# A fused transformer block on one core: the third normalisation moved out of the tokens and into the softmax

## The chip, the cores and the metric

The kernel runs on one core of one Trainium2 chip. Its time is the device time of one execution in microseconds (us). TensorE (PE in the profile, with PEld for its weight loads), VectorE (DVE), ScalarE (ACT), GpSimd (POOL) and SyncE (SP) run their own instruction streams and wait for each other by semaphores; only the DMA queues move data to and from memory.

## The reference, cut to what matters

Four residual steps on `x` of 4 x 2048 tokens x 512, all in fp32. The change concerns the third: attention of the normalised tokens to 77 context rows each sequence, with a ReLU projection on both sides.

```python
x = x + tanh(g_xattn[0]) * L0_xattn(ctx, layernorm(x), conv_w, conv_b, 1024, 1024, 4)
x = x + tanh(g_ffn[0]) * L0_ffn(layernorm(x), weight, bias)          # quantised linear layer
x = x + tanh(g_xattn[1]) * L1_xattn(layernorm(x), p_mask, ctx, q_mask, ctx, U_w, D_param)
x = x + tanh(g_ffn[1]) * L1_ffn(layernorm(x), Wr, W1, W2)            # 8 experts with a capacity

def layernorm(x, eps=1e-5):
    return (x - mean(x)) / sqrt(var(x) + eps)

def L1_xattn(passage, p_mask, question, q_mask, rep, U_w, D_param):
    Up = relu(einsum('bpi,hi->bph', passage, U_w))
    Uq = D_param[0] * relu(einsum('bqi,hi->bqh', question, U_w))
    scores = where(q_mask[:, None, :], -inf, einsum('bph,bqh->bpq', Up, Uq))
    return einsum('bpq,bqh->bph', softmax(scores, axis=2), rep)
```

## The kernel before

After a setup the kernel has two stages. The token stage (about 0 to 872 us) takes the tokens in 16 groups of 512 (four tiles of 128 tokens) through a pipeline of six stages, called z, a, b, c, d and e in the code. In one step the group of stage z is loaded, that of a is normalised and quantised (norms "a" and "b"), that of b goes through the quantised linear layer and gets the third norm (kind "c"), c is the attention projection with the scores, d the softmax and the attention's result, e the fourth norm (kind "d"), the router and the payload for the experts. The expert stage (872 us to the end) follows.

There are 21 steps. Steps 0 to 5 and 16 to 20 are written out, and steps 6 to 15 are a loop at run time (`Fori`, L210) on every engine. In the loop an address that turns with the group, such as a tile of `X`, comes from a register. Nothing schedules the kernel: each engine has a function `body(z, a, b, c, d, e)` in which the order of its work is written by hand, and every instruction waits for counters of others. A wait is a queue's head: what stands behind it on its engine waits too.

The places that the change touches, with their lines in this kernel:

- Third norm. VectorE takes `bn_stats` of each tile of `X` (`st_c`, L924), aggregates (`mv_c`, L928) and later makes the shift `nb_c` (L934). ScalarE makes `rs_c` by a logarithm `lv_c` (L555) and an exponential (L557), then writes four normalised tiles `n2` (L562; the profile calls this output `n`). TensorE turns `n2` by transposes against an identity (L718) in two pairs, and ScalarE and VectorE split the turned tiles into a high part `n2T_hi` (L574) and a low part `n2T_lo` (L1006).
- Linear layer. Four products of `wd` with the turned input `xdT` (TensorE, L710); VectorE adds each to `X` (`add_linear`, L974).
- Projection. Four products of `uw` with `n2T` (TensorE, L780), each relu'd by ScalarE into `up_hi` (`up(0)` to `up(3)`, L583), the low part `up_lo` by VectorE (L997).
- Softmax. VectorE takes the maximum `smx` over each row of scores (L1011) and subtracts it into `sc` (L1013), ScalarE takes one exponential over all four tiles, `al` (L601), TensorE turns it (L816), ScalarE and VectorE split it into `alT_hi` (L605) and `alT_lo`, and VectorE sums it into `ssm` (L1024) for the factor `scf`.
- GpSimd adds a bias to the whole group of `X` (L488), and SyncE loads the groups of `xs` and `X`.

`xs` is the shifted input of norm "a"; ScalarE writes its four normalised tiles (L638), which need `nb_a` (L1062) and the mask product `a_m` (L1059) of VectorE.

## Time and profile before

| | |
|---|---|
| Median of 3 runs | 2196.72 us (2196.54 to 2197.13) |
| The profiled execution, its own time | 2196.92 us |
| Its span (first to last instruction) | 2194.6 us |
| Mean granted TensorE clock | 0.961 |
| Busy: PE, PEld | 1982.1 us (90%), 1692.3 us (77%) |
| Busy: DVE, ACT, POOL | 1043.4 us (48%), 794.8 us (36%), 670.9 us (31%) |
| Token stage, then experts | 0 to 872 us, 872 to 2194.6 us |

The busy times are those of the whole span. The two stages have different limits, so they say little of one step of the token stage: for that the timeline of one step is read, engine by engine. All rows are of one execution.

### The profile page before, as it was taken

Reading aid. Unit: us, or ns where it says so; the run is one execution under the profiler, and the core shown is the slowest. Engines: PE = TensorE matmul, PEld = TensorE weight load, DVE = VectorE, ACT = ScalarE, POOL = GpSimd, SP = SyncE. Lnnn points to the kernel's source line nnn. Section 1 sums busy time; section 2 is a strip of 40 time slices with the busy share of each in tenths; the row PEclk is TensorE's granted clock in tenths of the full one; section 3 lists DMA queues with packets and bytes.
Section 4 is the critical chain, followed back from the end, with each engine's and each line's share of the span. In section 5 each row is a group of like instructions: output and inputs, shape, how many; then the busy total and the mean of one; then the engine's idle time right before and its main releaser. Section 6 shows DMA issues by size and latency. Waiting matters only on the chain.

```text
span 2194.6 us, 35464 instructions
## 1 busy us (share of the span) xinstructions
PE 1982.1 (90%) x11356; PEld 1692.3 (77%) x11357; DVE 1043.4 (48%) x2321; ACT 794.8 (36%) x1548; POOL 670.9 (31%) x579
## 2 busy tenths in 40 slices
PE   4468998899889975799999999999999999999997
PEld 2456776677667754698988998899889899899986
DVE  3478888998899744424241115122413313322241
ACT  1254656555665443324141114111413313311241
POOL 0534243434353302415051115111513313301250
PEclk9689999999999985899999999999999999999999
DMA  6311333333333423615051004201512403301130
GB/s 190 112 61 43 122 130 121 116 120 140 115 120 121 146 85 117 197 32 185 20 183 43 29 29 156 69 29 38 183 43 91 129 29 96 120 19 38 54 112 16
DMA packets 152243, 208.41 MB, mean 95 GB/s; under 512 B 12831, under 2 KB 78623, under 8 KB 152198
## 3 DMA queue, kind: packets, MB, share of 16 engines
q1 hardware_dynamic: 111125, 114.14, 16.3%
q0 software_dynamic: 15728, 43.38, 6.5%
q10 hardware_dynamic: 25344, 50.33, 6.3%
q8 instruction: 22, 0.36, 0.1%
q14 instruction: 24, 0.19, 0.0%
HBM read 140.98 MB, written 68.37 MB: 95 GB/s over the span
## 4 chain that ended last, share of the span: by engine, by line
PE 58%; ACT 0%; issue 0%; DMA 0%; POOL 0%; POOLq 0%; DVEq 0%; ACTq 0%; DVE 0%
PE bank L1646 23%; PE bank L1654 22%; PE bank L1619 5%; PE bank L1599 5%; PE bank L1577 1%; PE bank L1608 1%; DMA tg<-t_d,idx_t 0%; ACT w_hi L1510 0%; PE bank L1583 0%; ACT w_hi L1511 0%; POOLq L1351 0%; DMA slots<-slot_d 0%; POOL out_dram L1389 0%; DVEq L1292 0%; ACT inT_hi L1496 0%
## 5 line engine op out<-in xcount | busy, mean ns | idle before, releaser
L1737 DVE SCALAR_TENSOR_TENSOR hT_lo<-bank,hT_hi 128x256 fp32r<-128x256 f32 x352 | 149.0, 423 | 657.0 <-ACT hT_hi L1541 657.0
L1541 ACT ACTIVATE hT_hi<-bank 128x256 fp32r<-128x256 f32 x352 | 135.1, 384 | 747.8 <-PE bank L1646 747.8
L1646 PE MATMUL bank<-inT_hi,w_lo 128*128 128x256 f32 x1408 | 398.5, 283 | 0.0
L1646 PE MATMUL bank<-inT_lo,w_hi 128*128 128x256 f32 x1408 | 398.3, 283 | 0.0
L1646 PE MATMUL bank<-inT_hi,w_hi 128*128 128x256 f32 x1408 | 396.8, 282 | 0.0
L1654 PE MATMUL bank<-w_hi,hT_hi 128*128 128x512 f32 x704 | 279.9, 398 | 0.0
L1646 PEld LDWEIGHTS bank<-inT_hi,w_hi 128*128 128x128 f32 x1408 | 269.0, 191 | 13.3
L1646 PEld LDWEIGHTS bank<-inT_lo,w_hi 128*128 128x128 f32 x1408 | 269.0, 191 | 12.0
L1654 PE MATMUL bank<-w_lo,hT_hi 128*128 128x512 f32 x704 | 277.7, 394 | 0.0
L1654 PE MATMUL bank<-w_hi,hT_lo 128*128 128x512 f32 x704 | 274.1, 389 | 0.0
L1646 PEld LDWEIGHTS bank<-inT_hi,w_lo 128*128 128x128 f32 x1408 | 269.0, 191 | 0.0
L1389 POOL DMA_INDIRECT out_dram<-ob,idx_x x46 | 46.5, 1010 | 633.9 <-DVE ob L1747 617.5
L1399 POOL TENSOR_TENSOR w_lo<-stage,w_hi 128x512 fp32r<-128x512 f32 x112 | 159.9, 1444 | 79.8 <-ACT w_hi L1510 79.7
L1654 PEld LDWEIGHTS bank<-w_hi,hT_lo 128*128 128x128 f32 x704 | 132.3, 188 | 30.1
L1654 PEld LDWEIGHTS bank<-w_hi,hT_hi 128*128 128x128 f32 x704 | 133.5, 190 | 17.4
L1654 PEld LDWEIGHTS bank<-w_lo,hT_hi 128*128 128x128 f32 x704 | 133.6, 190 | 15.2
L718 PE MATMUL bank<-ident,n 128*128 128x128 f32 x512 | 79.8, 290 | 72.0 <-POOL n L494 40.3
L469 POOL DMA_INDIRECT slot_d<-pay,flat x64 | 62.6, 979 | 266.2 <-DVE flat L959 251.6
L494 POOL TENSOR_TENSOR n<-q,s 128x512 f32<-128x512 fp8e4 x64 | 83.5, 1332 | 188.0 <-DVE q L1108 188.0
L1711 DVE TENSOR_TENSOR w_lo<-stage,w_hi 128x512 fp32r<-128x512 f32 x128 | 133.3, 1054 | 0.0
L718 PEld LDWEIGHTS bank<-ident,n 128*128 128x128 f32 x512 | 59.9, 148 | 93.8 <-issue 66.1
L780 PE MATMUL bank<-n2T_hi,uw_hi 128*128 128x512 f32 x256 | 110.2, 430 | 13.3 <-DVE up_lo L997 13.3
(266 smaller groups left out, 3931.5 us busy)
## 6 DMA issues: line engine op xcount, KB each, us to landing
stage<-in_L_ffn_W_dram SPq DMA_DIRECT2D x256, 256.0 KB, 3.6
X<-in_x_dram SPq DMA_DIRECT2D x16, 1024.0 KB, 5.3
t_d<-tt ACTq DMA_DIRECT2D x16, 1024.0 KB, 4.4
x_d<-x ACTq DMA_DIRECT2D x16, 1024.0 KB, 6.7
out_dram<-y ACTq DMA_DIRECT2D x16, 1024.0 KB, 4.3
xs<-in_x_dram SPq DMA_DIRECT2D x16, 768.0 KB
cw_a<-in_L_xattn_conv_w_dram SPq DMA_DIRECT2D x2, 1024.0 KB, 17.1
cw_b<-in_L_xattn_conv_w_dram SPq DMA_DIRECT2D x2, 1024.0 KB, 18.8
```

Source lines behind the costliest of these rows:

```text
L469: pool.indirect_dma_start(out=slot_d, out_offset=bass.IndirectOffsetOnAxis(ap=flat[:, j:j + 1], axis=0), in_=pay[:, j, :], in_offset=None, ...
L494: pool.tensor_tensor(n1[:, j, :].rearrange("p (n c) -> p n c", c=BLK), q8[:, j, :].rearrange("p (n c) -> p n c", c=BLK), s64[:, j, :].unsq ...
L718: last = pe.transpose(dst_bank[:, k * P:k * P + P], src[:, j, k * P:k * P + P], ident[:, :])
L780: last = pe.matmul(u_banks[h % 2][:, :], l, rows_t, start=(k == 0 and n == 0), stop=(k == KB - 1 and n == 2))
L1399: pool.tensor_tensor(w1_lo[:, :, fs], w1_block(f), w1_hi[:, :, fs].bitcast(F32), ALU.subtract).then_inc(e_split[f % RING], 1)
L1541: act.activation(hT_hi[:, f % 4, :], hb[f % 4][:, 0:CN], ACT.Relu).then_inc(e_hh, 1)
L1599: last = pe.matmul(first_bank[q % 2][:, :], l[:, k, :], r[:, k, qs], start=(n == 0), stop=(n == 3 * KB - 1))
L1619: last = pe.matmul(unit_acc[:, :], l[:, q % 2, f, :], r[:, q * FQ + f, :], start=(q == 0 and n == 0), stop=(q == NF - 1 and n == 3 * FQ - 1))
L1646: last = pe.matmul(hb[f % 4][:, 0:CN], l[:, k, fs], r[:, k, :], start=(n == 0), stop=(n == 3 * KB - 1))
L1654: last = pe.matmul(acc[i][:, :], l[:, f % 4, js], r[:, f, :], start=(f == 0 and n == 0), stop=(f == FB - 1 and n == 2))
L1711: dve.tensor_tensor(w2_lo[:, f, :], w2_block(f), w2_hi[:, f, :].bitcast(F32), ALU.subtract).then_inc(e_split[f % RING], 1)
L1737: dve.scalar_tensor_tensor(out=hT_lo[:, f % 4, :], in0=hb[f % 4][:, 0:CN], scalar=0.0, in1=hT_hi[:, f % 4, :].bitcast(F32), op0=ALU.max, o ...
```

## The change

The kernel computes the same function by another route. A token's normalised row is (X - mean) * rs. The mean goes out of the tokens if every row of the projection weight is centred once: then `X` itself can be projected. The scale `rs` is positive, so it passes the ReLU and can be applied to the scores, in the exponential.

- Setup: ScalarE sums and centres the projection weight `uf`. The keys' side needs the uncentred weight, so TensorE sums the keys over the features (`keysum`) and VectorE adds the mean times that sum back, three instructions for each part instead of one. The mask's bias gets a factor that is zero where every key is masked.
- The third norm's `st_c`, `mv_c` and `nb_c` go. VectorE's `add_linear` also writes the sum of each row (`sum_c`), and one small instruction makes `nm_c`, the negative mean. ScalarE writes no `n2`: four squares of `X` with bias `nm_c` write their row sums `sq_c` (their full output goes to `junk`), and `lv_c` and `rs_c` follow these instead of standing ahead of `up(1)`.
- TensorE turns `X`, once all four `add_linear` are done; `x2T_hi` and `x2T_lo` take the place of `n2T`. Its loop over the steps is written out, that of the other engines isn't.
- Softmax: VectorE multiplies `smx` by -`rs_c` (`nbx`, 128x4) instead of subtracting; ScalarE's exponential reads the scores in four instructions of 128x77 with bias `nbx`, scale `rs_c` and the row sum `ssm` written by the way. TensorE waits for each tile. The router's product waits for the exponentials, not for VectorE.
- Scratch of the expert planner that lay in `n2` lies in `X`.

The diff, cut to its core:

```diff
@@ -144,12 +144,13 @@
-        for kind in "abcd":
+        for kind in "abd":
...
+        sum_c, nm_c, sq_c, rs_c = small("sum_c", T), small("nm_c", T), small("sq_c", T), small("rs_c", T * T)
...
-        smx, ssm, srd, scf = small("smx", T), small("ssm", T), small("srd", T), small("scf", T)
+        smx, nbx, ssm, srd, scf = (small(n, T) for n in ("smx", "nbx", "ssm", "srd", "scf"))
...
@@ -325,8 +328,8 @@
-        plan = n2[0:1, :, :].rearrange("o i d -> o (i d)")
-        onesc = n2[:, T - 1, 0:P]
+        plan = X[0:1, 0:T, :].rearrange("o i d -> o (i d)")
+        onesc = X[:, T - 1, 0:P]
...
@@ -537,7 +540,7 @@
-            pool.wait_ge(p_ct, T * NG)
+            pool.wait_ge(v_x3, T * (NG - T + 1))
             pool.iota(cidx, [[1, CI]], base=0, channel_multiplier=0,
...
@@ -597,8 +600,11 @@
-                    wait(act, v_sm, 4 * d + 2)
-                    act.activation(al[:, :, :], sc[:, :, :], ACT.Exp).then_inc(a_al, 1)
+                    wait(act, v_sm, 3 * d + 2)
+                    settled(act)
+                    for j in range(T):
+                        act.activation(al[:, j, :], p_sc[:, j, :], ACT.Exp, bias=nbx[:, j:j + 1],
+                                       scale=rs_c[:, ds((d % T) * T + j, 1)], accum_out=ssm[:, j:j + 1]).then_inc(a_al, 1)
                 if d is not None:
...
@@ -637,19 +643,26 @@
                                        scale=a_sc[:, j:j + 1]).then_inc(a_u, 1)
-                if b is not None:
-                    rstd("c", b)
                 up(1)
...
                 if b is not None:
-                    wait(act, v_ln["c"], LN * (b + 1))
-                    wait(act, p_ct, T * b)
-                    normed("c", n2, lambda j: X[:, ds((b % T) * T + j, 1), :], a_n2)
+
+                    wait(act, v_nm, b + 1)
+                    wait(act, a_sq, T * b)
+                    settled(act)
+                    for j in range(T):
+                        act.activation(junk[:, j, :], X[:, ds((b % T) * T + j, 1), :].rearrange("p o d -> p (o d)"),
+                                       ACT.Square, bias=nm_c[:, j:j + 1], accum_out=sq_c[:, j:j + 1]).then_inc(a_sq, 1)
+                    wait(act, a_sq, T * (b + 1))
+                    act.activation(lv["c"][:, :], sq_c[:, :], ACT.Ln, bias=eps[:, :], scale=1.0 / D).then_inc(a_rs["c"], 1)
+                    wait(act, a_rs["c"], 2 * b + 1)
+                    settled(act)
+                    act.activation(rs_c[:, ds((b % T) * T, T)], lv["c"][:, :], ACT.Exp, scale=-0.5).then_inc(a_rs["c"], 1)
                 up(3)
...
                     act.activation(re_[:, :, :], rd[:, :, :], ACT.Exp).then_inc(a_re, 1)
-                turned_hi(n2T_hi, n_banks, p_ct, b, a_ch, p_cu, 0, 2)
+                turned_hi(x2T_hi, n_banks, p_ct, b, a_ch, p_cu, 0, 2)
                 if e is not None:
...
@@ -679,6 +692,17 @@
             body(*groups(0))
+            act.wait_ge(ready, 1)
+            act.activation(onesr[:, :], onesf[:, :], ACT.Copy).then_inc(k_act, 1)
+            act.wait_ge(l_uf, 16)
+            for k in range(KB):
+                act.activation(uf[:, k, :], uf[:, k, :], ACT.Copy, accum_out=us[:, k:k + 1]).then_inc(k_act, 1)
+            act.wait_ge(k_act, act_at[f"us{KB - 1}"])
+            act.activation(unm[:, :], us[:, :], ACT.Copy, scale=-1.0 / D).then_inc(k_act, 1)
+            act.activation(umean[:, :], us[:, :], ACT.Copy, scale=1.0 / D).then_inc(k_act, 1)
+            act.wait_ge(k_act, act_at["unm"])
+            for k in range(KB):
+                act.activation(uf[:, k, :], uf[:, k, :], ACT.Identity, bias=unm[:, k:k + 1]).then_inc(k_act, 1)
             for k in range(KB):
...
@@ -758,7 +782,7 @@
-                        wait(pe, v_sm, 4 * d + 2)
+                        wait(pe, a_al, T * (d + 1))
...
@@ -776,7 +800,7 @@
-                                                                        n2T_hi[:, k, :], n2T_lo[:, k, :])):
+                                                                        x2T_hi[:, k, :], x2T_lo[:, k, :])):
...
@@ -786,12 +810,15 @@
                     if b is not None:
-                        wait(pe, a_n2, T * b + j + 1)
                         if j < 2:
-                            wait(pe, v_x2, T * b + 3 + j)
+                            wait(pe, v_x2, T * (b + 1))
                         else:
                             wait(pe, v_cl, T * b + j - 1)
-                        turn(n_banks[j % 2], n2, j).then_inc(p_ct, 1)
+                        for k in range(KB):
+                            last = pe.transpose(n_banks[j % 2][:, k * P:k * P + P],
+                                                X[:, (b % T) * T + j, k * P:k * P + P],
+                                                ident[:, :])
+                        last.then_inc(p_ct, 1)
...
@@ -811,8 +838,8 @@
                 if d is not None:
-                    wait(pe, a_al, d + 1)
                     for j in range(T):
+                        wait(pe, a_al, T * d + j + 1)
                         last = pe.transpose(b_s[0:L, j * P:j * P + P], al[:, j, :], ident[:, :])
...
@@ -888,6 +915,12 @@
+            pe.wait_ge(k_dve, dve_at["cxT3"])
+            for k in range(KB):
+                for c in (cxT_hi, cxT_lo):
+                    last = pe.matmul(bank[bank_of["keysum"]][:, 0:B * L], onesr[:, :], c[:, k, :],
+                                     start=(k == 0 and c is cxT_hi), stop=(k == KB - 1 and c is cxT_lo))
+            last.then_inc(k_pe, 1)
             for h in range(KB):
...
@@ -905,7 +938,8 @@
             prepared(pe)
-            pipeline(pe, body, 2)
+            for t in range(2, STEPS):
+                body(*groups(t))
...
@@ -971,8 +1005,10 @@
                     xb = tile_of(b, j).rearrange("p o d -> p (o d)")
+                    if j == 0:
+                        wait(dve, v_nm, b)
                     dve.scalar_tensor_tensor(out=xb, in0=l_banks[j % 2][:, :], scalar=gates[:, 2:3], in1=xb,
-                                             op0=ALU.mult, op1=ALU.add).then_inc(v_x2, 1)
+                                             op0=ALU.mult, op1=ALU.add, accum_out=sum_c[:, j:j + 1]).then_inc(v_x2, 1)
...
@@ -1009,9 +1045,11 @@
                     dve.tensor_reduce(smx[:, :], p_sc[:, :, :], AX.X, ALU.max).then_inc(v_sm, 1)
-                    wait(dve, v_sm, 4 * d + 1)
-                    dve.tensor_tensor(sc[:, :, :], p_sc[:, :, :], smx[:, :].unsqueeze(2).to_broadcast([P, T, L]),
-                                      ALU.subtract).then_inc(v_sm, 1)
+                    wait(dve, v_sm, 3 * d + 1)
+                    wait(dve, a_rs["c"], 2 * (d + 1))
+                    settled(dve)
+                    dve.scalar_tensor_tensor(out=nbx[:, :], in0=smx[:, :], scalar=-1.0, in1=rs_c[:, ds((d % T) * T, T)],
+                                             op0=ALU.mult, op1=ALU.mult).then_inc(v_sm, 1)
                 if e is not None:
...
@@ -1020,11 +1058,9 @@
                 if d is not None:
-                    wait(dve, a_al, d + 1)
-                    dve.tensor_reduce(ssm[:, :], al[:, :, :], AX.X, ALU.add).then_inc(v_sm, 1)
-                    wait(dve, v_sm, 4 * d + 3)
+                    wait(dve, a_al, T * (d + 1))
                     dve.reciprocal(srd[:, :], ssm[:, :]).then_inc(v_sm, 1)
-                    wait(dve, v_sm, 4 * d + 4)
+                    wait(dve, v_sm, 3 * d + 3)
                     dve.tensor_scalar(scf[:, :], srd[:, :], gx[:, ds(d, 1)], None, ALU.mult).then_inc(v_scf, 1)
...
@@ -1063,11 +1099,10 @@
                     wait(dve, v_x2, T * (b + 1))
-                    moments("c", b, lambda j: tile_of(b, j))
+                    wait(dve, a_sq, T * b)
+                    dve.tensor_scalar(nm_c[:, :], sum_c[:, :], -1.0 / D, None, ALU.mult).then_inc(v_nm, 1)
                 add_attention(3)
                 up_rest(1)
-                if b is not None:
-                    shift("c", b)
                 if e is not None:
...
@@ -1194,8 +1226,12 @@
                 dve.wait_ge(k_pe, pe_at[f"uq{h}"])
-                step(f"uqf{h}", dve.tensor_scalar(uqf[:, h, :], bank[bank_of[f"uq{h}"]][:, 0:B * L], 0.0,
-                                                  dp[:, h:h + 1], ALU.max, ALU.mult))
+                step(f"uqm{h}", dve.tensor_scalar(uqf[:, h, :], bank[bank_of["keysum"]][:, 0:B * L], umean[:, h:h + 1],
+                                                  None, ALU.mult))
+                after(f"uqm{h}")
+                step(f"uqa{h}", dve.tensor_tensor(uqf[:, h, :], bank[bank_of[f"uq{h}"]][:, 0:B * L], uqf[:, h, :], ALU.add))
+                after(f"uqa{h}")
+                step(f"uqf{h}", dve.tensor_scalar(uqf[:, h, :], uqf[:, h, :], 0.0, dp[:, h:h + 1], ALU.max, ALU.mult))
             low_parts("wd", wd_hi, wd_lo, D)
```

In the order of each engine's instructions this moves rows at three places. The first is ScalarE in a written-out step ahead of the loop, from norm "a" to the turned tiles (`X`, `xs` are the group's tiles, `bank` a PSUM bank). Before:

```order
L557 ACTIVATE rs_a<-lv_a 128x4
L638 ACTIVATE xs<-xs,nb_a,a_sc 128x512 x4
L555 ACTIVATE lv_c<-mv_c,eps 128x4
L557 ACTIVATE rs_c<-lv_c 128x4
L583 ACTIVATE up_hi<-bank 128x512 x2
L562 ACTIVATE n<-X,nb_c,rs_c 128x512 x4
L583 ACTIVATE up_hi<-bank 128x512
```

The same place of ScalarE after the change:

```order
L560 ACTIVATE rs_a<-lv_a 128x4
L644 ACTIVATE xs<-xs,nb_a,a_sc 128x512 x4
L586 ACTIVATE up_hi<-bank 128x512 x2
L654 ACTIVATE junk,sq_c<-X,nm_c 128x512 x4
L657 ACTIVATE lv_c<-sq_c,eps 128x4
L660 ACTIVATE rs_c<-lv_c 128x4
L586 ACTIVATE up_hi<-bank 128x512
```

The logarithm and the exponential moved from ahead of the second and third `up_hi` to ahead of the fourth, and the squares stand where the normalisations stood.

The second is VectorE in the same step, from norm "a" to the quantisation. Before:

```order
L1062 SCALAR_TENSOR_TENSOR nb_a<-mv_a,a_m 128x4
L924 BN_STATS st_c<-X 128x6 x4
L928 BN_AGGR mv_c<-st_c 128x2 x4
L987 SCALAR_TENSOR_TENSOR x<-bank,scf,X 128x512
L997 SCALAR_TENSOR_TENSOR up_lo<-bank,up_hi 128x512
L934 SCALAR_TENSOR_TENSOR nb_c<-mv_c,rs_c 128x4
L997 SCALAR_TENSOR_TENSOR up_lo<-bank,up_hi 128x512
L1095 TENSOR_REDUCE ab<-n 128x16 x4
```

The same place of VectorE after:

```order
L1098 SCALAR_TENSOR_TENSOR nb_a<-mv_a,a_m 128x4
L1103 TENSOR_SCALAR nm_c<-sum_c 128x4
L1023 SCALAR_TENSOR_TENSOR x<-bank,scf,X 128x512
L1033 SCALAR_TENSOR_TENSOR up_lo<-bank,up_hi 128x512 x2
L1130 TENSOR_REDUCE ab<-n 128x16 x4
```

Eight instructions on `X` became one of 128x4, and the shift is gone: nothing is left between the second and the third `up_lo`.

The third is VectorE at the softmax, at the start of a step. Before:

```order
L1011 TENSOR_REDUCE smx<-bank 128x4
L1013 TENSOR_TENSOR sc<-bank,smx 128x308
L924 BN_STATS st_d<-x 128x6 x4
L928 BN_AGGR mv_d<-st_d 128x2 x4
L1020 TENSOR_TENSOR alT_lo<-bank,alT_hi 77x512
L974 SCALAR_TENSOR_TENSOR X<-bank,gates,X 128x512
L1024 TENSOR_REDUCE ssm<-al 128x4
L1026 RECIPROCAL srd<-ssm 128x4
```

The same place of VectorE after:

```order
L1047 TENSOR_REDUCE smx<-bank 128x4
L1051 SCALAR_TENSOR_TENSOR nbx<-smx,rs_c 128x4
L958 BN_STATS st_d<-x 128x6 x4
L962 BN_AGGR mv_d<-st_d 128x2 x4
L1058 TENSOR_TENSOR alT_lo<-bank,alT_hi 77x512
L1010 SCALAR_TENSOR_TENSOR X,sum_c<-bank,gates,X 128x512
L1062 RECIPROCAL srd<-ssm 128x4
```

A 128x4 product took the place of the subtraction, the row sum went to ScalarE, and `add_linear` got its second output.

## Rows read from the trace of the kernel before

**Rows 1.** Busy time by stretch: start:end, length, busy (xinstructions), clock, DMA share, GB/s.

```profile
300.00:698.00 398.00, 356.59 (x1917) 281.88 (x1917) 354.20 (x889) 242.37 (x432) 163.92 (x90) 1.00 0.35 123
872.00:2194.60 1322.60, 1284.56 (x7800) 1144.07 (x7800) 388.84 (x657) 349.68 (x754) 367.18 (x388) 0.99 0.26 81
```

**Rows 2.** Timeline of VectorE, one step: start, length, instruction [idle before <-releaser].

```profile
425.20 0.69 DVE L997 SCALAR_TENSOR_TENSOR up_lo<-bank,up_hi 128x512 fp32r<-128x512 f32 x1
...
436.53 0.47 DVE L1011 TENSOR_REDUCE smx<-bank 128x4 f32<-128x308 f32 x1
437.03 0.48 DVE L1013 TENSOR_TENSOR sc<-bank,smx 128x308 f32<-128x308 f32 x1
...
458.17 1.82 DVE L1059 TENSOR_TENSOR a_m<-rs_a,mg 128x4 f32<-128x4 f32 x1 [0.77 <-ACT rs_a L557]
...
460.38 2.47 DVE L924 BATCH_NORM_STATS2 st_c<-X 128x6 f32 x4
462.77 0.41 DVE L928 BATCH_NORM_AGGREGATE mv_c<-st_c 128x2 f32<-128x6 f32 x4
...
464.87 0.15 DVE L934 SCALAR_TENSOR_TENSOR nb_c<-mv_c,rs_c 128x4 f32<-128x4 f32 x1
...
469.46 0.69 DVE L997 SCALAR_TENSOR_TENSOR up_lo<-bank,up_hi 128x512 fp32r<-128x512 f32 x1
```

**Rows 3.** Timeline of TensorE in the same step.

```profile
435.55 0.49 PE L710 MATMUL bank<-wd_hi,xdT_hi 128*128 128x512 f32 x1
...
438.40 0.60 PE L816 MATMUL bank<-ident,al 128*77 128x128 f32 x4
438.75 0.48 PE L710 MATMUL bank<-wd_hi,xdT_hi 128*128 128x512 f32 x1
...
464.05 0.40 PE L780 MATMUL bank<-n2T_hi,uw_lo 128*128 128x512 f32 x1
```

**Rows 4.** Timeline of ScalarE in the same step.

```profile
437.54 0.46 ACT L601 ACTIVATE al<-sc 128x308 f32<-128x308 f32 x1 [1.91 <-DVE sc L1013]
...
448.65 0.81 ACT L562 ACTIVATE n<-X,nb_b,rs_b 128x512 f32 x1 [1.20 <-DVE nb_b L934]
...
460.38 2.94 ACT L638 ACTIVATE xs<-xs,nb_a,a_sc 128x512 f32<-128x512 f32 x4 [2.41 <-DVE nb_a L1062]
463.22 0.29 ACT L555 ACTIVATE lv_c<-mv_c,eps 128x4 f32<-128x4 f32 x1
463.54 0.20 ACT L557 ACTIVATE rs_c<-lv_c 128x4 f32<-128x4 f32 x1
463.65 0.58 ACT L583 ACTIVATE up_hi<-bank 128x512 fp32r<-128x512 f32 x1
464.48 0.60 ACT L583 ACTIVATE up_hi<-bank 128x512 fp32r<-128x512 f32 x1 [0.25 <-PE bank L780]
465.29 2.94 ACT L562 ACTIVATE n<-X,nb_c,rs_c 128x512 f32 x4 [0.21 <-DVE nb_c L934]
468.13 0.57 ACT L583 ACTIVATE up_hi<-bank 128x512 fp32r<-128x512 f32 x1
```

**Rows 5.** Waits from 345 to 698 us: who for whom, us in total, times, longest.

```profile
DVE up_lo L997 <- ACT up_hi L583: 21.4, 16, 2.4
```

**Rows 6.** Timeline of GpSimd in the same step.

```profile
455.39 4.56 POOL L488 TENSOR_TENSOR X<-X,gbias 128x2048 f32 x1
```

**Rows 7.** ScalarE and VectorE in the first of the two last steps with a projection.

```profile
730.46 2.92 ACT L562 ACTIVATE n<-X,nb_c,rs_c 128x512 f32<-128x512 f32 x4
...
733.89 0.69 DVE L997 SCALAR_TENSOR_TENSOR up_lo<-bank,up_hi 128x512 fp32r<-128x512 f32 x1
```

**Rows 8.** VectorE in the third step of the pipeline.

```profile
119.77 2.46 DVE L924 BATCH_NORM_STATS2 st_c<-X 128x6 f32<-128x512 f32 x4
...
123.35 1.86 DVE L1095 TENSOR_REDUCE ab<-n 128x16 f32<-128x512 f32 x3
```

**Rows 9.** VectorE at the end of the setup.

```profile
86.06 2.47 DVE L924 BATCH_NORM_STATS2 st_a<-xs 128x6 f32<-128x512 f32 x4 [9.43 <-DMA xs<-comp_d]
```

49 lines of the change are left out of this document (27 added, 22 removed).

## The prediction

> **What bounds the kernel now.** I read three views: busy time by stretch, the chain of waits in the steady stretch, and the timeline of one step, engine by engine. By stretch [rows 1] the change can only act ahead of 872 us: the experts behind it take 1322.6 us at a clock of 0.99, and none of their instructions is touched. In the stretch 300 to 698 TensorE is busy 356.6 and VectorE 354.2 of 398 us, so neither is alone the bound; a step has to be followed round.
>
> A step takes 44.26 us: the fourth `up_lo` of a step starts at 425.20 and again at 469.46 [rows 2]. The same work can be followed as a ring. TensorE starts the first linear product at 435.55 and goes on without a wait of note through the four linear products, the attention and projections 0 to 2; the last matmul of projection 2 starts at 464.05 and its bank is full at 464.45 [rows 3]. ScalarE then writes `up_hi` at 464.48, the four normalised tiles at 465.29 (2.94 us) and the last `up_hi` at 468.13, done at 468.70 [rows 4]. VectorE writes the last `up_lo` at 469.46 [rows 2], 0.76 us after that was ready, since VectorE itself came late. Behind it stand the quantisation and the low parts, 10.3 us until TensorE starts the next step. So the ring is TensorE, then VectorE, with ScalarE 0.76 us behind being the bound. VectorE has slack elsewhere: for earlier `up_hi` it waits on ScalarE 16 times in 8 steps, 21.4 us, at the longest 2.4 [rows 5].
>
> **The change, part by part.** Each sum is for one step.
>
> *Moments of the third norm (VectorE).* Removed: four statistics (2.47 us), four aggregates (0.41 us) and the shift (0.15 us); added is one 128x4 instruction of about 0.15. That is 2.8 us less on VectorE between 460.38 and 464.87 [rows 2]. It is nearly all hidden: what VectorE does next needs the second `up_hi`, and ScalarE reaches that only after its four `xs` instructions (460.38 to 463.32 [rows 4]), which themselves wait for `a_m`. `a_m` cannot come earlier either: it is a 128x4 instruction of 1.82 us that ends at 459.99, when GpSimd's 4.56 us addition ends at 459.95 [rows 2, 6]. VectorE gains the 0.45 us of `lv_c` and `rs_c`, which move behind the third `up_hi`, and the shift. So VectorE could start the last `up_lo` about 0.5 us earlier, and the question is whether ScalarE lets it.
>
> *Squares, logarithm and exponential (ScalarE).* The four normalisations become four squares with a bias pointer, a number as scale, and an accumulated sum. Start to start a normalisation takes 0.71 ((2.94 - 0.81)/3, 0.81 being one's length [rows 4]). A pointer operand costs 0.09: `lv_c` with a bias takes 0.29, `rs_c` without takes 0.20 [rows 4]. So a square is 0.62, plus the accumulated sum, call it r. No row shows r. From below it is 0; from above 0.32, the distance from `lv_c` to the `rs_c` that depends on it [rows 4]. The nearest row is a small instruction behind another: `rs_c` starts 0.11 before the `up_hi` that follows it. I take r = 0.13, because reading a sum must wait for the last column. From the third `up_hi` to the last there now lie 0.49 + 3 x 0.75 + (0.71 + 0.13) for the squares, 0.34 for the logarithm, 0.35 for the exponential with its wait, less 0.10 of overlap: 4.17 us, where it was 3.65. That is +0.52.
>
> In the Trainium skill, "ScalarE: Activation LUTs", section What ACT_TABLE_LOAD costs, a pointer operand adds about 93 ns and back-to-back instructions overlap by about 93 ns; this trace agrees, with 0.09 and 0.10. "VectorE: DVE Perf Modes", section Two Vector instructions with no wait between them, says of the other engine that an instruction which also writes its accumulator is two instructions; no run here shows it yet, and it speaks for an r above nothing.
>
> *Exponential of the scores.* Before, `smx` ends at 437.00, `sc` at 437.51, ScalarE's one 128x308 `al` runs from 437.54 to 438.00, and TensorE takes it at 438.40, 0.4 us later [rows 2 to 4]. The subtraction goes (0.48 us), a 128x4 product comes (0.15 us, behind two waits, until about 437.3), and `al` becomes four 128x77 instructions with two pointers and a sum. The first starts about 0.27 after its release, as the normalisation at 465.29 does after the `nb_c` that ends at 465.02 [rows 2, 4], because its operand is addressed by a register: 437.56. One takes 0.20 + 77 x (0.46 - 0.20)/304 + 2 x 0.09 = 0.45, start to start 0.35 + r = 0.48. The fourth ends at 437.56 + 1.44 + 0.58 = 439.58. TensorE's last transpose of the four then starts near 439.7 and the second linear product near 439.8, where it was 438.75 [rows 3]: +1.07 us on TensorE, on the ring. The sum over the rows that VectorE saves lies in its slack, and is worth nothing.
>
> *TensorE turns X itself.* The first two turnings no longer wait for ScalarE's normalised tiles; in a steady step they stand behind projection 3 in TensorE's order and TensorE has no wait there, so nothing is gained. Projection 3 still waits for the second `up_lo`, now earlier than TensorE arrives. TensorE's loop is written out. The trace of before shows no such thing in the loop, but a wait that needs a register took 0.27 (above) where `al` followed `sc` in 0.03 [rows 2, 4]; TensorE may win between 0 and 0.24 for each wait that is late. I take 0.1 on the ring.
>
> *The sum of a steady step.* The last `up_hi` starts at 464.48 + 1.07 + 4.17 = 469.72, `up_lo` at 469.72 + 0.58 + 0.03 = 470.33 instead of 469.46: +0.87, less 0.1 for the written-out waits and less 0.07 for what VectorE need not catch up, +0.7. There are eleven such steps (ten of the loop and about one of the written-out ones ahead of it): +7.7.
>
> *The last two steps with a projection.* Without a first stage, VectorE waits for nobody else: the normalised tiles start at 730.46 and the last `up_lo` at 733.89, right behind its `up_hi` [rows 7]. Here all of 1.07 + 0.52 counts: 2 x 1.6 = +3.2.
>
> *The first steps.* In the third step of the pipeline there is no projection, so the moments stand on the path: `st_c` at 119.77, `ab` at 123.35 [rows 8]. That goes but for one small instruction: -3.4. The next gives -0.4.
>
> *The setup.* ScalarE sums and centres the projection weight (eight 128x512 and three small instructions: 8 x 0.6 + 3 x 0.2 = 5.4 us by the lengths in [rows 4]), TensorE adds 8 matmuls, VectorE 8 instructions of 128x308 and two small ones, 3.8 us on VectorE for the eight at the 0.48 of `sc` [rows 2]. VectorE idles 9.43 us ahead of 86.06 for a transfer that none of it feeds [rows 9]. I put it at nothing; with that cover gone it would be +4.
>
> Together 7.7 + 3.2 - 3.4 - 0.4 = +7.1 us on the profiled execution, which took 2196.9 (its span is 2194.6); the median of the runs is 2196.7, so I forecast 2203.8.
>
> **Rivals.** *The sum is nearly free.* If r is 0.02, the exponentials end 0.55 us earlier and the squares take 0.55 less: 1.1 us a step, and the steady step is shorter by 0.4 us. Eleven steps give -4.4, the last two +1.0, the first two -3.8: 2189.7, faster. For it: nothing but that a sum rides along with the data; against it, every instruction in the rows costs at least 0.1. It decides below r = 0.05.
>
> *Even.* With r near 0.08 the steady step gains or loses 0.3 at most and the last steps pay back what the first ones won: some 2199 us, within the 0.2% (4.4 us) that a measurement of this kernel can tell. For it: the nearest row, 0.11, is close.
>
> *The read drains the engine.* If the sum waits for its instruction to end and is then an instruction of 0.2 itself, with the overlap lost, r is 0.2 to 0.3. Each 0.1 more costs 0.4 in the exponentials and 0.4 in the squares: thirteen steps x 0.8 = +10 us per 0.1. At r = 0.2 the kernel takes 2211, at 0.3 2221. The row for it is the 0.32 from `lv_c` to `rs_c`.
>
> *The moments matter after all.* If ScalarE could run ahead, VectorE's 2.8 us a step would be worth up to 13 x 2.5 = 32 us. The rows of ScalarE and GpSimd [rows 4, 6] speak against it: the four `xs` wait for GpSimd.
>
> **How the numbers follow.** The forecast (r from 0.09 to 0.16, 2200 to 2208) 0.36, a dearer read 0.21, even 0.22, nearly free 0.17, the last 0.04. Slower by over 0.2% is the forecast's and the dearer read's, 0.55; within it 0.25, with a part of the forecast's low end; faster 0.20. The range 2189 to 2214 leaves out the ends of the dearest and of the last rival.
>
> **What would show it.** In the steady step: ScalarE's four `al` ending near 439.6 in the old step's count, TensorE waiting 1 us ahead of them; the squares 0.75 apart; VectorE waiting for the last `up_hi` instead of being late; a step of about 45.0 us. A gap of under 0.65 between squares would make the forecast wrong, as would a step under 44.3. The step from 93 to 127 us should shrink by 3.4, and 86.06 should stand. If the two last steps don't grow, the logarithm and exponential are not where I put them.

## The result and the profile after

| | before | after |
|---|---|---|
| Median of the runs | 2196.63 us (2196.30 to 2197.13, 4 runs) | 2211.78 us (2208.61 to 2213.12, 4 runs) |
| Span of the profiled execution | 2194.6 us | 2211.4 us |
| Mean granted clock | 0.961 | 0.959 |

The ratio is 1.0067, with a 95% interval of 1.0049 to 1.0084: slower by 15 us, clear of noise. 2203.8 was forecast, with a range of 2189 to 2214.

The step's marks tell where the time went. VectorE computes the reciprocal `i` once in each step, right behind the last `up_lo`; the table gives its start, and for the last three steps that of ScalarE's `sT`.

| stretch | before, us | after, us | difference | forecast |
|---|---|---|---|---|
| start to the first `i` | 92.53 | 99.47 | +6.94 | 0 |
| the next two steps, which had the statistics on the path | 71.88 | 68.57 | -3.31 | -3.8 |
| the last two written-out steps and the first of the loop | 128.59 | 132.51 | +3.92 | +1.4 (two of the eleven steady ones) |
| nine steps of the loop | 398.36 | 404.70 | +6.34 | +6.3 |
| the last three with a projection | 125.47 | 128.75 | +3.28 | +3.2 |
| the rest, experts included | 1377.77 | 1377.40 | -0.4 | 0 |

The steady step, the first two steps and the end came out nearly as forecast. The miss is in the setup and in two written-out steps.

One thing has to be taken out of single steps first, TensorE's granted clock. Three stretches from one `i` to the next, first one of the kernel before, then two of the changed kernel (start:end, length, busy time of PE, PEld, DVE, ACT and POOL, clock, DMA share, GB/s):

```profile
246.91:293.00 46.09, 41.31 (x213) 32.39 (x213) 39.43 (x101) 27.70 (x50) 18.42 (x10) 0.96 0.34 115
```

```profile
345.47:390.62 45.15, 40.78 (x213) 32.54 (x213) 35.70 (x96) 28.28 (x60) 18.22 (x10) 0.96 0.34 117
390.62:435.53 44.91, 40.17 (x213) 31.35 (x213) 35.60 (x95) 28.28 (x60) 18.24 (x10) 1.00 0.34 118
```

A step whose clock is 0.96 has some 4 us at about the lower of TensorE's two levels (1.2 GHz; 353.5 to 357.5 in the second fence) and is longer for it. TensorE's waits ahead of that are the same as in the next step, which kept the full clock (1.67, 0.80, 0.49 and 1.15 us in both), so no wait ahead of it explains the drop. The nine steady steps have none of these before the change and two after it. At the full clock a step takes 44.26 before and 44.91 after: +0.65; the mean of all nine is 0.70 longer.

**The steady step.** VectorE's timeline (start, length, instruction), one step of the changed kernel, against [rows 2]:

```profile
479.83 0.69 DVE L1033 SCALAR_TENSOR_TENSOR up_lo<-bank,up_hi 128x512 fp32r<-128x512 f32 x1 [0.66 <-ACT up_hi L586]
...
491.15 0.47 DVE L1047 TENSOR_REDUCE smx<-bank 128x4 f32<-128x308 f32 x1
492.12 0.16 DVE L1051 SCALAR_TENSOR_TENSOR nbx<-smx,rs_c 128x4 f32<-128x4 f32 x1 [0.51 <-DVE smx L1047]
...
515.39 0.17 DVE L1103 TENSOR_SCALAR nm_c<-sum_c 128x4 f32<-128x4 f32 x1
...
518.87 0.69 DVE L1033 SCALAR_TENSOR_TENSOR up_lo<-bank,up_hi 128x512 fp32r<-128x512 f32 x1 [2.36 <-ACT up_hi L586]
...
524.74 0.69 DVE L1033 SCALAR_TENSOR_TENSOR up_lo<-bank,up_hi 128x512 fp32r<-128x512 f32 x1 [0.66 <-ACT up_hi L586]
```

The step takes 44.91 us, where it was 44.26. VectorE now waits for the last `up_hi` (0.66 us), where it came late before. The statistics are gone, and in their place VectorE waits 2.36 us ahead of the second `up_lo`. The waits in the same stretch say it in one line (total, times, longest), against 21.4 us in 16 waits [rows 5]:

```profile
DVE up_lo L1033 <- ACT up_hi L586: 41.3, 23, 2.4
```

TensorE and ScalarE in this step, against [rows 3, 4]:

```profile
490.09 0.50 PE L734 MATMUL bank<-wd_hi,xdT_hi 128*128 128x512 f32 x1 [0.20 <-DVE x2T_lo L1042]
...
493.10 1.53 PE L843 MATMUL bank<-ident,al 128*77 128x128 f32 x4
494.38 0.48 PE L734 MATMUL bank<-wd_hi,xdT_hi 128*128 128x512 f32 x1
...
519.64 0.39 PE L804 MATMUL bank<-x2T_hi,uw_lo 128*128 128x512 f32 x1
```

```profile
475.15 0.60 ACT L586 ACTIVATE up_hi<-bank 128x512 fp32r<-128x512 f32 x1 [1.24 <-PE bank L804]
475.65 0.71 ACT L654 ACTIVATE junk<-X,nm_c 128x512 f32 x1
476.26 0.19 ACT L654 ACTIVATION_READ_ACCUMULATOR junk<-X,nm_c 128x1 f32 x1
...
478.60 0.30 ACT L657 ACTIVATE lv_c<-sq_c,eps 128x4 f32<-128x4 f32 x1
479.10 0.20 ACT L660 ACTIVATE rs_c<-lv_c 128x4 f32 x1 [0.20 <-ACT lv_c L657]
479.21 0.59 ACT L586 ACTIVATE up_hi<-bank 128x512 fp32r<-128x512 f32 x1
...
492.54 0.42 ACT L606 ACTIVATE al<-bank,nbx,rs_c 128x77 f32<-128x77 f32 x1 [2.29 <-DVE nbx L1051]
...
492.95 0.41 ACT L606 ACTIVATE al<-bank,nbx,rs_c 128x77 f32<-128x77 f32 x1
...
493.73 0.41 ACT L606 ACTIVATE al<-bank,nbx,rs_c 128x77 f32<-128x77 f32 x1
494.03 0.21 ACT L606 ACTIVATION_READ_ACCUMULATOR al<-bank,nbx,rs_c 128x1 f32 x1
```

From the first to the second linear product TensorE takes 4.29 us instead of 3.20: +1.09. From the third `up_hi` to the fourth ScalarE takes 4.06 instead of 3.65: +0.41. The last `up_lo` starts 0.62 behind the start of its `up_hi` instead of 1.33: -0.71. TensorE starts 10.26 us behind the last `up_lo` instead of 10.35 (-0.09), and needs 25.65 from the second linear product to the end of projection 2 instead of 25.70 (-0.05). Together +0.65. The row sum is an instruction of its own, 0.19 us long, and adds some 0.09 to the distance of two squares (0.71 for one pointer and a sum, where 0.62 was worked out for one pointer alone).

**The setup.** VectorE and GpSimd:

```profile
64.18 0.48 DVE L1232 TENSOR_TENSOR uqf<-bank,uqf 128x308 f32<-128x308 f32 x1
64.69 7.17 DVE L1234 TENSOR_SCALAR uqf<-uqf,dp 128x308 f32<-128x308 f32 x1
...
72.86 0.38 DVE L1234 TENSOR_SCALAR uqf<-uqf,dp 128x308 f32<-128x308 f32 x1
...
85.25 2.46 DVE L958 BATCH_NORM_STATS2 st_b<-X 128x6 f32<-128x512 f32 x4
...
88.84 2.47 DVE L958 BATCH_NORM_STATS2 st_a<-xs 128x6 f32<-128x512 f32 x4
...
92.30 4.26 DVE L1095 TENSOR_TENSOR a_m<-rs_a,mg 128x4 f32<-128x4 f32 x1 [0.66 <-ACT rs_a L560]
```

```profile
58.17 5.05 POOL L532 TENSOR_TENSOR cx_hl<-cx,cx_hl 77x512 fp32r<-77x512 f32 x4 [54.92 <-ACT cx_hl L714]
63.18 4.05 POOL L536 TENSOR_TENSOR wf<-wq,wsc 128x512 f32<-128x512 fp8e4 x4
67.20 4.49 POOL L483 TENSOR_TENSOR X<-X,xs 128x2048 f32<-128x2048 f32 x1
...
92.05 4.49 POOL L491 TENSOR_TENSOR X<-X,gbias 128x2048 f32<-128x2048 f32 x1 [20.36 <-ACT n L565]
```

One 128x308 instruction with input and output in SBUF took 7.17 us; the same instruction took 0.38 when GpSimd was idle. It ends at 71.86, when GpSimd's chain, busy without a gap since 58.17, ends at 71.69; it was not let in at 67.20 either, where one GpSimd instruction follows another. The instruction ahead of it, which reads PSUM, took its 0.48 beside the same chain. VectorE thus comes to `st_a` at 88.84, with nothing left of the 9.43 us for which it waited for the transfer [rows 9]. There the product `a_m` falls beside GpSimd's next addition (92.05 to 96.54), which is late itself since it waited for ScalarE's `n` behind `st_b`, and is held until 96.56. Of the 6.94 us, 2.78 are the late `st_a` (88.84 against 86.06) and some 4.1 the held `a_m`, which took 0.16 before.

**The written-out steps.** In the first step with a softmax the new product `nbx`, again all in SBUF, meets GpSimd too (VectorE's row, then GpSimd's):

```profile
178.23 1.35 DVE L1051 SCALAR_TENSOR_TENSOR nbx<-smx,rs_c 128x4 f32<-128x4 f32 x1 [0.17 <-DVE smx L1047]
...
174.96 4.60 POOL L483 TENSOR_TENSOR X<-X,xs 128x2048 f32<-128x2048 f32 x1
```

It ends at 179.58, GpSimd at 179.56: 1.2 us longer than its 0.16. In the next step it has 1.01 us, 0.85 longer. From the first to the second linear product TensorE takes 5.25 us in the one step, where it was 3.23, and 4.82 in the other, where it was 3.24: +2.02 and +1.58. That is the 1.09 of the steady step without the 0.33 us by which `nbx` starts later there (0.50 against 0.17 behind `smx`), and with the 1.2 and the 0.85.

What is left of +2.56 and +2.27 differs between the two. In the second step it is ScalarE's squares: from the third `up_hi` to the fourth 3.99 us instead of 3.32. In the first step the squares cost nothing, since the fourth `up_hi` waits for its bank anyway. There projection 3 is slower, behind a wait of TensorE of 3 us that it had before too. TensorE and ScalarE in the changed kernel, with the clock of that stretch:

```profile
204.35 0.80 PE L804 MATMUL bank<-x2T_hi,uw_hi 128*128 128x512 f32 x1 [3.00 <-DVE up_lo L1033]
209.87 0.60 ACT L586 ACTIVATE up_hi<-bank 128x512 fp32r<-128x512 f32 x1 [2.34 <-PE bank L804]
```

```profile
204.35:209.83 5.48, 5.48 (x13) 4.26 (x14) 3.10 (x6) 3.02 (x10) 0.00 (x0) 0.50 0.25 96
```

The twelve matmuls take 5.48 us at the lower clock from end to end (0.50). Before, behind a wait of 3.43 us, they took 4.63 (199.02 to 203.65), at 0.52 for the first 3.58 and at 1.00 from there: +0.85. The second `up_lo`, for which TensorE waits there, comes 0.32 us sooner against the second linear product, so 2.02 + 0.85 - 0.32 = 2.55, and measured is 2.56. The slower clock is no work of the change: `e7_before_unrolled`, which doesn't have it, takes 41.40 us in this step, where the kernel before took 40.51, and has the same 0.92 over it (0.96 before). Why the clock came back later is open.

The first step of the loop is 0.91 shorter than before (45.18 against 46.09), but it was the kernel before that had the low clock in it (0.96 above); `e7_before_unrolled`, where only TensorE's loop is written out, takes 44.89 there at 1.00. So this 0.91 is no gain of the change.

In the Trainium skill, "SBUF — State Buffer", section Who interferes with whom, the rule is that a VectorE instruction in a mode with two ports, or with two SBUF inputs, and a GpSimd instruction that reads SBUF take a shared pair of ports one after the other, the first for its whole length; a VectorE instruction with at most one input in SBUF, outside those modes, does not contend. This case's rows agree: 7.17 and 0.38 us for the one form, 0.48 for the other, which has one input in PSUM.

### The profile page after: what moved, and what is told of

Its sections match the earlier page's. It is cut to its first block, busy times and chain, and to the rows that moved or that the text cites. A ratio compares the mean times of both kernels' runs of the same rounds, so it can differ in the third digit from the quotient of the medians.

```text
span 2211.4 us, 35349 instructions
## 1 busy us (share of the span) xinstructions
PE 1999.4 (90%) x11364; PEld 1700.5 (77%) x11365; DVE 1007.2 (46%) x2250; ACT 821.0 (37%) x1739; POOL 664.3 (30%) x579
## 4 chain that ended last, share of the span: by engine, by line
PE 58%; ACT 0%; issue 0%; DMA 0%; POOL 0%; POOLq 0%; DVEq 0%; ACTq 0%; DVE 0%
PE bank L1687 23%; PE bank L1695 22%; PE bank L1660 5%; PE bank L1640 5%; PE bank L1618 1%; PE bank L1649 1%; DMA tg<-t_d,idx_t 0%; PE bank L1624 0%; ACT w_hi L1552 0%; ACT w_hi L1551 0%; POOLq L1392 0%; DMA slots<-slot_d 0%; POOL out_dram L1430 0%; DVEq L1333 0%; ACT inT_hi L1537 0%
## 5 line engine op out<-in xcount | busy, mean ns | idle before, releaser
L804 PE MATMUL bank<-x2T_hi,uw_hi 128*128 128x512 f32 x256 | 109.6, 428 | 6.7 <-DVE up_lo L1033 6.7
L734 PE MATMUL bank<-wd_hi,xdT_hi 128*128 128x512 f32 x256 | 106.2, 415 | 2.1 <-DVE x2T_lo L1042 2.1
L804 PE MATMUL bank<-x2T_lo,uw_hi 128*128 128x512 f32 x256 | 103.4, 404 | 0.0
```

The lines of the kernel that those rows point to most:

```text
L734: last = pe.matmul(dst, l, r, start=(n == 0), stop=(n == len(terms) - 1))
L804: last = pe.matmul(u_banks[h % 2][:, :], l, rows_t, start=(k == 0 and n == 0), stop=(k == KB - 1 and n == 2))
```

## The experiments

Each row is one kernel: the ratio to the kernel before with its 95% interval, and of its profiled execution the start of the first `i`, the five steps from there, the mean of the nine steady steps, the mean of those that had a granted clock of 1.00 (and how many), and the span.

| kernel | ratio | first `i` | next five | steady step | at clock 1.00 | span |
|---|---|---|---|---|---|---|
| before | 1 | 92.53 | 200.47 | 44.26 | 44.26 (9) | 2194.6 |
| after | 1.0067 [1.0049, 1.0084] | 99.47 | 201.08 | 44.97 | 44.91 (7) | 2211.4 |
| e1_uq_psum | 1.0041 [1.0027, 1.0055] | 93.16 | 199.32 | 45.01 | 44.94 (7) | 2205.3 |
| e2_moments_back | 1.0036 [1.0024, 1.0049] | 98.46 | 201.21 | 44.39 | 44.31 (7) | 2203.6 |
| e3_squares_spread | 1.0021 [1.0011, 1.0031] | 97.74 | 197.53 | 44.36 | 44.18 (5) | 2199.1 |
| e4_turn_al_later | 1.0123 [1.0106, 1.0140] | 98.53 | 200.94 | 46.45 | 46.32 (7) | 2223.9 |
| e5_uq_and_squares | 1.0001 [0.9992, 1.0010] | 93.38 | 198.83 | 44.15 | 44.15 (9) | 2194.1 |
| e6_one_exp | 1.0016 [1.0007, 1.0025] | 93.11 | 197.71 | 44.72 | 44.69 (8) | 2199.3 |
| e7_before_unrolled | 0.9993 [0.9984, 1.0002] | 92.38 | 200.93 | 44.34 | 44.28 (8) | 2196.0 |
| e8_exp_no_sum | 1.0045 [1.0030, 1.0060] | 98.61 | 199.07 | 44.56 | 44.56 (9) | 2203.7 |
| e9_up_split | 0.9988 [0.9979, 0.9997] | 93.20 | 196.44 | 44.28 | 44.14 (6) | 2192.6 |
| e10_split_no_sum | 0.9979 [0.9970, 0.9988] | 93.14 | 195.67 | 44.19 | 44.19 (9) | 2190.3 |
| e11_split_one_exp | 1.0005 [0.9996, 1.0014] | 92.80 | 194.93 | 44.69 | 44.66 (8) | 2196.0 |
| e12_squares_last | 0.9965 [0.9951, 0.9978] | 92.76 | 192.57 | 44.37 | 44.03 (4) | 2189.7 |

The low clock belongs to the execution, not to the edit, as far as these traces tell: e3 and e5 have the same loop, and e3's trace has four such steps, e5's none. The steps are therefore compared at 1.00.

Theory: the loss is the held instruction in the setup (6.3 us) plus a steady-step loss on two places of the ring, TensorE's wait for the four exponentials and ScalarE's squares, logarithm and exponential. Its rival for the setup: the centring and the extra matmuls are late by themselves. For the step: VectorE's statistics were on the path after all, or the loss is only one of the two places.

### The held instruction (e1_uq_psum)

```diff
-                step(f"uqa{h}", dve.tensor_tensor(uqf[:, h, :], bank[bank_of[f"uq{h}"]][:, 0:B * L], uqf[:, h, :], ALU.add))
+                step(f"uqa{h}", dve.tensor_tensor(bank[bank_of[f"uq{h}"]][:, 0:B * L], bank[bank_of[f"uq{h}"]][:, 0:B * L],
+                                                  uqf[:, h, :], ALU.add))
                 after(f"uqa{h}")
-                step(f"uqf{h}", dve.tensor_scalar(uqf[:, h, :], uqf[:, h, :], 0.0, dp[:, h:h + 1], ALU.max, ALU.mult))
+                step(f"uqf{h}", dve.tensor_scalar(uqf[:, h, :], bank[bank_of[f"uq{h}"]][:, 0:B * L], 0.0,
+                                                  dp[:, h:h + 1], ALU.max, ALU.mult))
```

> The changed kernel, but in the setup the sum for the keys is written back to its PSUM bank and the ReLU and scale read it there, instead of all three instructions keeping it in SBUF. Same count, same sizes. Theory A (one VectorE instruction with SBUF on both sides, which took 7.17 us, was held while GpSimd worked; that is what the setup cost): it takes about 0.54 us, VectorE reaches the norm of the first group about 6.7 us sooner, and the first quantisation, 6.94 us late against the kernel before, is at most 2 us late; the total falls by 5 to 7 us, to about 2206. Rival B (the setup is late through ScalarE's centring and the extra matmuls, and the long instruction only filled a wait): the first quantisation stays 6 to 7 us late and the total stays at 2211 to 2213.

VectorE's rows at the same place:

```profile
63.28 0.54 DVE L1235 TENSOR_SCALAR uqf<-bank,dp 128x308 f32<-128x308 f32 x1
...
74.96 2.46 DVE L958 BATCH_NORM_STATS2 st_b<-X 128x6 f32<-128x512 f32 x4
...
86.69 2.47 DVE L958 BATCH_NORM_STATS2 st_a<-xs 128x6 f32<-128x512 f32 x4 [8.09 <-DMA xs<-comp_d]
```

0.54 us instead of 7.17, `st_b` 10.3 us sooner, and the wait for the transfer is back with 8.09 us. The first `i` is 0.63 late instead of 6.94. Theory A holds. The first `i` varies by itself: in the five traces with the held instruction it starts at 97.74 to 99.47, so 5.2 to 6.9 us late, and in the seven without it at 92.76 to 93.38. The centring, the sums and the extra matmuls cost at most 0.9. The steady step did not change (44.94).

### The statistics back on VectorE (e2_moments_back)

```diff
-                    dve.tensor_scalar(nm_c[:, :], sum_c[:, :], -1.0 / D, None, ALU.mult).then_inc(v_nm, 1)
+                    for j in range(T):
+                        dve.bn_stats(ln["c"][0][:, j, :], tile_of(b, j)).then_inc(v_ln["c"], 1)
+                    for j in range(T):
...
+                        dve.bn_aggr(ln["c"][1][:, j, :], ln["c"][0][:, j, :]).then_inc(v_ln["c"], 1)
...
-                    for j in range(T):
-                        act.activation(junk[:, j, :], X[:, ds((b % T) * T + j, 1), :].rearrange("p o d -> p (o d)"),
-                                       ACT.Square, bias=nm_c[:, j:j + 1], accum_out=sq_c[:, j:j + 1]).then_inc(a_sq, 1)
-                    wait(act, a_sq, T * (b + 1))
-                    act.activation(lv["c"][:, :], sq_c[:, :], ACT.Ln, bias=eps[:, :], scale=1.0 / D).then_inc(a_rs["c"], 1)
+                    act.activation(lv["c"][:, :], ln["c"][1][:, :, 1], ACT.Ln, bias=eps[:, :]).then_inc(a_rs["c"], 1)
```

> The changed kernel, but the variance of the third norm comes from VectorE's statistics again, as before; the squares and row sums go, the logarithm and exponential stay ahead of the last projection's ReLU, and the softmax is as changed. Theory A (of the steady step's +0.65, ScalarE's squares hold the last ReLU 0.4 us longer and VectorE then waits for it; VectorE's own 2.9 us for the statistics lie where it waited 2.4 us for the second ReLU): the last ReLU starts at once behind its bank, VectorE comes late instead, and a step takes 44.2 to 44.6 instead of 44.91; total 2204 to 2209. Rival B (the relief of VectorE was worth something in the step): a step gets longer, 45.2 or more, total 2216 or more.

ScalarE, then VectorE, at the end of a step:

```profile
475.39 0.60 ACT L587 ACTIVATE up_hi<-bank 128x512 fp32r<-128x512 f32 x1 [1.64 <-PE bank L798]
```

```profile
467.91 2.47 DVE L1097 BATCH_NORM_STATS2 st_c<-X 128x6 f32 x4
...
471.55 0.68 DVE L1025 SCALAR_TENSOR_TENSOR up_lo<-bank,up_hi 128x512 fp32r<-128x512 f32 x1
...
476.67 0.69 DVE L1025 SCALAR_TENSOR_TENSOR up_lo<-bank,up_hi 128x512 fp32r<-128x512 f32 x1
```

With 2.9 us of work given back to VectorE the steady step is 0.60 us shorter than in the changed kernel (44.31 against 44.91), because ScalarE is free of the squares and the last `up_hi` waits for its bank alone. Theory A. So moving the moments from VectorE to ScalarE was itself a loss at this place.

### The squares elsewhere (e3_squares_spread)

```diff
                 up(1)
+                squares(0, 2)
                 up(2)
-                if b is not None:
...
-                    for j in range(T):
-                        act.activation(junk[:, j, :], X[:, ds((b % T) * T + j, 1), :].rearrange("p o d -> p (o d)"),
...
+                squares(2, T)
                 up(3)
...
                 turned_hi(x2T_hi, n_banks, p_ct, b, a_ch, p_cu, 0, 2)
+                if b is not None:
+                    wait(act, a_sq, T * (b + 1))
+                    act.activation(lv["c"][:, :], sq_c[:, :], ACT.Ln, bias=eps[:, :], scale=1.0 / D).then_inc(a_rs["c"], 1)
```

> The changed kernel with ScalarE's order altered alone: two squares stand behind the second ReLU of the projection, two behind the third, and the logarithm and exponential behind the first turned tiles. Theory A (the squares, logarithm and exponential between the third and fourth ReLU are on the path): the fourth ReLU starts about 1.3 us sooner, the last low part then comes 0.65 us sooner, bound by VectorE's block maxima; a step takes 44.25 to 44.35 instead of 44.91; total 2202 to 2205. Rival B (the path runs through TensorE's later start alone, and ScalarE has slack): a step stays at 44.8 to 45.0 and the total within 2 us of the changed kernel.

```profile
469.74 0.19 ACT L654 ACTIVATION_READ_ACCUMULATOR junk<-X,nm_c 128x1 f32 x1
470.63 0.60 ACT L586 ACTIVATE up_hi<-bank 128x512 fp32r<-128x512 f32 x1 [0.71 <-PE bank L810]
```

ScalarE's last `up_hi` waits 0.71 for TensorE's bank; before, it waited for nothing but the squares. The steady step falls by 0.73 to 44.18, somewhat more than theory A said, and the ratio from 1.0067 to 1.0021, some 10 us: theory A. (Of these 10 us, 1.7 are an earlier first `i`, which this edit doesn't touch.) Since nothing behind the third norm needs `rs_c` before the softmax two steps later, the squares can stand anywhere; that is what the change makes possible and did not use.

### TensorE's order (e4_turn_al_later)

```diff
                 linear(0)
+                linear(1)
                 if d is not None:
                     for j in range(T):
                         wait(pe, a_al, T * d + j + 1)
...
-                linear(1)
-                attend(0)
                 linear(2)
+                attend(0)
```

> The changed kernel with TensorE's order altered: the four exponentials are turned behind the second linear product instead of ahead of it, the first attention product stands behind the third linear product, and VectorE adds the first linear product before the low part of the exponentials. Theory A (TensorE waits 1.1 us a step for the four exponentials, and that is most of the loss): the wait goes, the projections start about 1 us sooner and a step takes 43.8 to 44.2; total 2199 to 2203. Rival B (the wait moves: the attention, or the fourth norm's tiles behind it, come late by as much): a step of 44.8 or more, total 2210 or more.

```profile
494.95 0.50 PE L734 MATMUL bank<-wd_hi,xdT_hi 128*128 128x512 f32 x1 [0.21 <-DVE x2T_lo L1042]
...
500.53 0.60 PE L844 MATMUL bank<-ident,al 128*77 128x128 f32 x4
...
506.25 0.49 PE L734 MATMUL bank<-cxb,alT_hi 77*128 77x512 f32 x1 [0.68 <-DVE x L1023]
```

```profile
501.26 0.59 ACT L611 ACTIVATE alT_hi<-bank 77x512 fp32r<-77x512 f32 x1 [2.15 <-PE bank L844]
```

The wait for the exponentials went, but two linear products take 5.6 us (494.95 to 500.53), and the exponentials were there before: ScalarE waited 2.15 us for the turned bank (0.5 in the changed kernel), and the attention and the fourth norm behind it came late. The steady step is 46.32, the slowest of all: rival B.

### Both edits (e5_uq_and_squares)

The edits of the first and the third experiment together.

> The changed kernel with both edits that worked: the keys' sum back in PSUM in the setup, and ScalarE's squares spread behind the second and third ReLU. Theory A (the two losses are separate: 6.3 us in the setup, 0.6 to 0.7 in each of some thirteen steps): the first quantisation is at most 1 us late against the kernel before, a steady step takes 44.2 to 44.4; total 2195 to 2199. Rival B (what the setup gives is taken back, since the first steps wait for something else): 2200 to 2203.

First `i` at 93.38, steady step 44.15, ratio 1.0001. The two losses are separate, and without them nothing is left of the slowdown, though TensorE still waits for the four exponentials (4.30 us from the first to the second linear product). The change, with its two flaws mended, is worth nothing measurable on the kernel before.

### One exponential (e6_one_exp)

```diff
+                    dve.tensor_tensor(sc[:, :, :], p_sc[:, :, :], smx[:, :].unsqueeze(2).to_broadcast([P, T, L]),
+                                      ALU.subtract).then_inc(v_sm, 1)
...
+                    dve.tensor_tensor(sc[:, :, :], sc[:, :, :],
+                                      rs_c[:, ds((d % T) * T, T)].unsqueeze(2).to_broadcast([P, T, L]),
+                                      ALU.mult).then_inc(v_sm, 1)
...
-                    for j in range(T):
-                        act.activation(al[:, j, :], p_sc[:, j, :], ACT.Exp, bias=nbx[:, j:j + 1],
-                                       scale=rs_c[:, ds((d % T) * T + j, 1)], accum_out=ssm[:, j:j + 1]).then_inc(a_al, 1)
+                    act.activation(al[:, :, :], sc[:, :, :], ACT.Exp).then_inc(a_al, 1)
```

> The last kernel, with the exponential as one 128x308 instruction of ScalarE: VectorE subtracts the maximum and multiplies by the token's scale (two 128x308 instructions), and sums the rows again. Theory A (TensorE's wait for four exponentials of 0.39 each is on the path): the last exponential ends about 2.0 us behind the maximum instead of 2.5, TensorE's second linear product starts 0.4 to 0.6 us sooner, a steady step takes 43.7 to 43.9, total 2190 to 2194. Rival B (the path now runs through VectorE, which gets 1.3 us more work a step): a step of 44.2 or more and a total equal to or above that of the last kernel.

TensorE starts the second linear product 2.81 us behind the start of `smx` (480.49 to 483.30) instead of 3.23 (479.52 to 482.75 in the kernel that it builds on): 0.42 us sooner. Yet the steady step grows from 44.15 to 44.69: rival B. What is later is `flat`, a small instruction of VectorE for which GpSimd waits: it starts 24.64 us behind `i` (469.78 to 494.42) instead of 24.09 (468.80 to 492.89). What follows is rigid. GpSimd and then VectorE in this kernel:

```profile
495.44 1.01 POOL L473 DMA_INDIRECT slot_d<-pay,flat  x1 [14.32 <-DVE flat L997]
...
500.30 4.57 POOL L492 TENSOR_TENSOR X<-X,gbias 128x2048 f32 x1
...
503.01 1.89 DVE L1105 TENSOR_TENSOR a_m<-rs_a,mg 128x4 f32<-128x4 f32 x1 [0.77 <-ACT rs_a L561]
```

Four slot writes, the addition until 504.87, `a_m` held until 504.90, then ScalarE's four tiles and the second `up_hi`, then VectorE to the end of the step. From `flat` to the next `i` it takes 20.05 us, and 20.04 in the kernel it builds on, so the 0.55 us of `flat` come out as 0.54 of the step. This is a second ring, VectorE to `flat`, GpSimd, ScalarE, VectorE, and by these rows it binds once the squares are out of the way, not TensorE's.

### TensorE's loop written out (e7_before_unrolled)

```diff
-            pipeline(pe, body, 2)
+            for t in range(2, STEPS):
+                body(*groups(t))
```

> The kernel before, with TensorE's loop over the steps written out and nothing else changed. Theory A (as forecast: TensorE's late waits no longer fetch a register): a steady step takes 44.0 to 44.2 instead of 44.26, total 1 to 3 us under the kernel before. Rival B (nothing on the path, and more code to fetch): a step of 44.26 to 44.5, total equal or up to 3 us above.

Steady step 44.28 against 44.26, ratio 0.9993 with 1 inside the interval. No gain of 0.1 a step: rival B in the step, and nothing measurable in the total.

### No row sum on ScalarE (e8_exp_no_sum)

```diff
-                                       scale=rs_c[:, ds((d % T) * T + j, 1)], accum_out=ssm[:, j:j + 1]).then_inc(a_al, 1)
+                                       scale=rs_c[:, ds((d % T) * T + j, 1)]).then_inc(a_al, 1)
...
+                    dve.tensor_reduce(ssm[:, :], al[:, :, :], AX.X, ALU.add).then_inc(v_sm, 1)
```

> The changed kernel, where the four exponentials write no row sum and VectorE sums their rows as before. Theory A (the accumulator's read costs about 0.09 in the distance of two instructions of ScalarE): the four start 0.30 to 0.33 apart instead of 0.39, the last ends 0.3 us sooner, a steady step takes 44.6 to 44.7 instead of 44.91; total 2208 to 2210. Rival B (the read is hidden behind the next instruction's start, and the distance is that of instructions with two pointers): 0.38 to 0.40 apart, the step and the total as in the changed kernel.

```profile
488.05 1.33 ACT L606 ACTIVATE al<-bank,nbx,rs_c 128x77 f32<-128x77 f32 x4 [2.30 <-DVE nbx L1051]
```

Four in 1.33 us, so (1.33 - 0.42)/3 = 0.30 apart instead of 0.39: a row sum costs 0.09 here too. The steady step falls by 0.35 to 44.56. Theory A, and a little more than the 0.3 us of the exponentials.

### Towards a faster kernel (e9 to e12)

`e9_up_split` builds on both edits and puts the second ReLU between the tiles of norm a:

```diff
                     for j in range(T):
+                        if j == 2:
+                            up(1)
                         act.activation(xs[:, j, :], xs[:, j, :], ACT.Identity, bias=ln["a"][3][:, j:j + 1],
```

> The kernel with both edits that worked (keys' sum in PSUM, squares spread), with one more change of ScalarE's order: the second ReLU of the projection stands between the second and third normalised tile of norm a, not behind all four. Theory A (with the squares out of the way VectorE's order sets the end of the step: it starts the last low part 0.5 us behind the ReLU that it needs, since its own chain starts with the second low part, which waited 2.4 us for ScalarE): the second low part comes 1.2 us sooner, the last stands right behind its ReLU, a steady step takes 43.6 to 43.8 instead of 44.15, total 2190 to 2194. Rival B (TensorE and ScalarE bound the step as well, within 0.1): a step of 44.1 and a total as in the kernel without it, 2197 to 2199.

The steady step stays (44.14 against 44.15, rival B): the second low part came sooner, but VectorE then waited 1.29 us for the third ReLU, which two squares hold. The five steps before gain 2.4 us. Ratio 0.9988.

`e10_split_no_sum` adds to this the edit of e8, `e11_split_one_exp` that of e6.

> The same kernel, where the four exponentials write no row sum and VectorE sums the rows. Theory A (with VectorE's chain relieved TensorE sets the step, and its wait for the exponentials is on the path): the last exponential ends 0.3 us sooner, a steady step is 0.2 to 0.35 shorter than with the sums on ScalarE, total 3 us less. Rival B (VectorE still binds, and the 0.47 us of its sum cancels the gain): the same step or up to 0.2 longer.

Ratio 0.9979 with an interval to 0.9988: 0.2% faster than the kernel before. But the steady step is 44.19, where it was 44.14: rival B. TensorE's wait for the exponentials is not what binds here.

> The same kernel with one 128x308 exponential, the subtraction, the scaling and the sum on VectorE. Theory A (as in the last one: TensorE's wait is what counts, and here it is 0.6 us less): a steady step of 43.1 to 43.4, total 2186 to 2190. Rival B (VectorE binds, as it did when this was tried without the moved ReLU: 44.69 against 44.15): a step of 43.8 or more.

Step 44.66, 0.52 more than in e9 and the same loss as without the moved ReLU: rival B, as the second ring would have it, where VectorE's 0.55 us ahead of `flat` count in full. No run changes GpSimd's part of that ring; it is read from the rows above.

`e12_squares_last` builds on e10 and moves ScalarE's squares once more:

```diff
-                squares(0, 2)
                 up(2)
-                squares(2, T)
+                squares(0, 2)
                 up(3)
...
                 turned_hi(xdT_hi, q_banks, p_bt, a, a_bh, p_bm, 2, T)
+                squares(2, T)
+                if b is not None:
+                    wait(act, a_sq, T * (b + 1))
+                    act.activation(lv["c"][:, :], sq_c[:, :], ACT.Ln, bias=eps[:, :], scale=1.0 / D).then_inc(a_rs["c"], 1)
```

> The best kernel so far (keys' sum in PSUM, second ReLU between the tiles of norm a, no row sums on ScalarE), with ScalarE's squares put elsewhere again: two between the third and fourth ReLU, two with the logarithm and exponential at the very end of the step. Theory A (its steady step of 44.19 is set by a ring of GpSimd's addition, the mask product held by it, ScalarE's tiles and the two squares ahead of the third ReLU, for which VectorE waited 1.29 us): the third ReLU starts at least 1 us sooner, a steady step takes 43.6 to 43.9, total 2187 to 2191. Rival B (TensorE's bank for the third ReLU is full no sooner, or the squares at the end hold up the exponentials by as much): a step of 44.1 to 44.3 and a total of 2193 to 2196.

```profile
458.20 0.60 ACT L586 ACTIVATE up_hi<-bank 128x512 fp32r<-128x512 f32 x1 [1.04 <-PE bank L813]
...
475.61 1.33 ACT L606 ACTIVATE al<-bank,nbx,rs_c 128x77 f32<-128x77 f32 x4 [0.46 <-issue]
```

The third `up_hi` now waits 1.04 us for TensorE's bank, which is full no sooner, and the squares at the end delay the exponentials, which start 0.82 us behind the end of `nbx` (474.79) instead of 0.26. Both are what rival B named. These rows are from steps with the low clock, of which this trace has five in nine; in the other four the delay is 0.57 and the step takes 44.03, 0.16 less than in e10. The third `up_hi` starts 39.59 us behind the `i` before it, where e10 has 39.77, and its bank is full at 39.55, where e10 has 39.26. So the edit shortens the step a little, by less than theory A asked (43.6 to 43.9). The total is the lowest, ratio 0.9965 [0.9951, 0.9978], 0.35% under the kernel before. More than all of it comes from the first steps: the five take 192.57 us instead of 200.47 (some 1.2 of it the low clock in the trace of before, by e7's 44.89 for its 46.09), and in the profiled execution, whose span is 4.9 us under that of before, the nine steady steps, with their five at the low clock, give 1.0 back and the last three 2.0. What bounds the steady step at 44.0 to 44.2 when neither the squares nor `flat` are in the way was not separated; two kernels with different orders end there. By the rows, in e12 it is TensorE's bank for the third `up_hi`, and in e10 it isn't.

## Why the prediction was right, and where it was not

The direction and the range held; the centre was 8 us low. By its own steps:

- *The moments are hidden.* Right. VectorE waits 2.36 us where the statistics stood, and giving it the work back cost nothing (44.31 in e2 against 44.91). The reason named, ScalarE's four `xs` behind `a_m` behind GpSimd's addition, is part of the second ring that e6 and e11 point to.
- *Squares, logarithm, exponential: +0.52.* Measured +0.41 from the third to the fourth `up_hi`. The sum of a row was put at 0.13 and is 0.09; e3 took the whole term out.
- *The exponentials: +1.07.* Measured +1.09, but as two errors that cancel. The distance of two was put at 0.48 and is 0.39: 0.30 without the sum (e8), where 0.35 was worked out, and the sum 0.09 instead of 0.13. The start of the first was put at 0.56 behind the end of `smx` and is 0.92, since `nbx` starts 0.50 behind `smx` in the loop, and not at once. In the written-out steps this distance is 0.17.
- *TensorE's written-out loop: -0.1.* Not shown to be anything: 44.28 against 44.26 (e7).
- *The steady step: +0.7.* Measured +0.65 at the full clock, +0.70 as the mean of nine. The first ones: -3.8, measured -3.3.
- *The last steps: +3.2.* Measured +3.3, by luck. Two steps were counted at 1.6 each; there are three, with +1.23, +1.35 and +0.70. The last has a projection and a softmax but no squares.
- *The setup: nothing.* The step that failed, with 6.94 us. It took the eight added instructions at 0.48 each, 3.8 us on VectorE, inside the 9.43 us of slack, and its own sign, that 86.06 should stand, failed (88.84). What it missed was shown in its own rows: a 128x4 product of 1.82 us that ends with GpSimd's addition [rows 2, 6]. The prediction used that to say when `a_m` can end, and did not ask which new instructions of VectorE have the same form. Four of the setup's twelve have it, input and output in SBUF; the first fell beside GpSimd's chain of 13.5 us and lost 6.8 us until its end.
- *The steps in between.* One of the two written-out steps was not counted, the other taken as a steady one. In both, `nbx` was held by GpSimd for 1.2 and 0.85 us, the same cause as in the setup. The rest is the squares in the one, and in the other projection 3 at the lower clock, which no term had and which isn't the change's. The loop's first step, 0.91 shorter, took part of it back in this trace, and that was the clock as well.

Of the rivals none came about. The total, 2211.8, is the figure of the dearer read (2211 at r = 0.2), but r is 0.09: it came from the setup and the two written-out steps, not from the read. The nearly free rival was priced against its own rates: at 0.4 us for each 0.1 of r in either place, r = 0.02 is worth 0.44 + 0.44 a step and not 1.1, which puts the steady step at -0.2 and not at -0.4. The row sum's 0.09 lies at the lower end of the forecast's own case (0.09 to 0.16), and with it alone, eight sums 0.04 us cheaper, the steady step would have come to +0.4; the late start of the first exponential made up the rest.

## What to carry to other kernels

An instruction that a change adds is priced by its form as well as its size: if one row of the trace shows a small VectorE instruction that ends exactly when a GpSimd instruction ends, look for every new one with the same operands, and keep one operand in PSUM where GpSimd is busy. Relief of an engine is worth nothing at a place where it then waits; find the ring, and put moved work where the ring does not pass. Before a difference of some tenths between two steps is explained, their granted clocks are compared. A term taken from the steady loop is counted anew for the steps that fill the pipeline, where another engine is late.

## What the runs showed of the hardware

- A row sum written by an ScalarE instruction appears as an instruction of its own, 0.19 to 0.21 us, of which 0.09 shows in the distance to the next: 0.39 against 0.30 for 128x77 (after, e8). On VectorE it is 0.08 us long, one for each `add_linear`.
- A 128x308 VectorE instruction from SBUF to SBUF: 0.38 us alone, 7.17 us beside GpSimd (7.64, 8.10, 7.18 and 7.38 in e2, e3, e4 and e8), across the seam of two GpSimd instructions; reading PSUM, 0.54, in all four of e1, beside GpSimd's chain (57.31 to 70.90).
- In the loop, where the address and the counts that it waits for come from registers, `nbx` started 0.50 us behind the end of `smx`; in the written-out steps 0.17. Whether the address or the wait does it was not separated.
- Some 4 us of a step at a granted clock of about half (0.96 over the step) make a steady step 0.2 to 0.7 us longer here: 45.15 against 44.91 (after), 44.60 against 44.18 (e3), 44.72 against 44.03 (e12). In e3's trace it is four of the nine steady steps, in e5's, with the same loop, none.
